# Rows of three graphs by index transfers through HBM instead of one-hot matmuls, in a graph-attention and mixture-of-experts kernel

## The reference, cut to what matters

```python
def per_graph(x, a):                       # 4 graphs of 256 rows; a = layernorm(x), 256 x 256
    h = gat_layer(x, a, W0, ...)           # twice: feat = x W; softmax(leaky(e) - 1e10*(1-a)) @ feat; + b; elu
    return gat_layer(h, a, W1, ...)
x = x + tanh(g_xattn) * gat(ctx, layernorm(x))
# then a mixture of experts over the 1024 rows of layernorm(x):
logits = tanh(xt @ Wg1.T) @ Wg2.T          # 8 experts, the best 2 weighted by a softmax
h = silu(einsum('td,ehd->teh', xt, Wup) + bup)
out = einsum('te,teo->to', scores, einsum('teh,eoh->teo', h, Wdown) + bdown)
x = x + tanh(g_ffn) * out
```

## Time and profile before

| | before |
|---|---|
| time, median of 3 runs | 93.43 us (92.78 to 94.61) |
| profiled execution: its time | 93.16 us |
| profiled execution: its span | 91.4 us |
| PE busy, PEld busy | 83.3 us (91%), 78.1 us (85%) |
| DVE, ACT, POOL busy | 64.7 us (71%), 55.2 us (60%), 43.5 us (48%) |
| share of PE in the chain that ended last | 59%; DVE 17%, DMA 6%, issue 6%, ACT 5% |

### The profile page before, as it was taken

One profiled execution on the slowest core, in us unless ns is written; L12 is line 12 of the kernel. 1 busy time (PEld: TensorE's weight loads), 2 busy tenths in 40 slices (PEclk: granted clock), 3 DMA queues, 4 the chain that ended last, 5 costly groups with the idle time before them and its releaser, 6 DMA issues.

```text
span 91.4 us, 1958 instructions
## 1 busy us (share of the span) xinstructions
PE 83.3 (91%) x615; PEld 78.1 (85%) x615; DVE 64.7 (71%) x202; ACT 55.2 (60%) x132; POOL 43.5 (48%) x95
## 2 busy tenths in 40 slices
PE   4959999989999999999999999999999999999800
PEld 4728888869899999989998999999999999999700
DVE  5887797857897609998599368795359767899520
ACT  1446888596695948398927799763366564433100
POOL 7970953698003999925900002885002988800000
PEclk9999999999999999999999999999999999999998
DMA  1999991000000000000000000030000030003021
GB/s 34 286 273 400 405 386 60 0 0 0 7 4 0 0 0 0 7 0 4 0 0 0 7 0 0 4 115 4 7 0 0 0 115 0 0 7 115 4 84 56
DMA packets 3339, 5.44 MB, mean 60 GB/s; under 512 B 474, under 2 KB 2748, under 8 KB 3068
## 3 DMA queue, kind: packets, MB, share of 16 engines
q1 hardware_dynamic: 3164, 5.00, 16.0%
q10 hardware_dynamic: 160, 0.26, 1.1%
HBM read 4.21 MB, written 1.05 MB: 58 GB/s over the span
## 4 chain that ended last, share of the span: by engine, by line
PE 59%; DVE 17%; DMA 6%; issue 6%; ACT 5%; DVEq 1%; POOL 1%; ACTq 1%
PE bank L734 6%; DMA ctx_sb<-in_ctx_t 6%; PE bank L735 6%; PE bank L739 6%; PE bank L896 6%; PE bank L781 5%; PE bank L872 5%; PE bank L783 5%; PE bank L782 5%; DVE hid_lo L1093 4%; PE bank L859 3%; PE bank L756 3%; DVE hid L1085 2%; PE bank L679 2%; DVE stat L990 2%
## 5 line engine op out<-in xcount | busy, mean ns | idle before, releaser
L1085 DVE TENSOR_TENSOR hid<-act_sb,bank 128x256 f32<-128x256 f32 x32 | 13.4, 418 | 10.9 <-PE bank L756 9.0
L518 ACT ACTIVATE act_sb<-bank,small_sb 128x256 f32<-128x256 f32 x32 | 15.1, 471 | 8.7 <-PE bank L739 8.4
L526 ACT CAST hid_hi<-hid 128x256 fp32r<-128x256 f32 x32 | 13.0, 405 | 10.7 <-DVE hid L1085 9.7
L781 PE MATMUL bank<-wdown_hi,hid_hi 128*128 128x256 f32 x64 | 18.4, 287 | 0.3 <-ACT hid_hi L526 0.3
L734 PE MATMUL bank<-xt_hi,wup_hi 128*128 128x256 f32 x64 | 18.0, 304 | 0.1
L783 PE MATMUL bank<-wdown_hi,hid_lo 128*128 128x256 f32 x64 | 18.1, 282 | 0.0
L782 PE MATMUL bank<-wdown_lo,hid_hi 128*128 128x256 f32 x64 | 18.0, 281 | 0.0
L735 PE MATMUL bank<-xt_hi,wup_lo 128*128 128x256 f32 x64 | 16.6, 281 | 0.0
L1093 DVE TENSOR_TENSOR hid_lo<-hid,hid_hi 128x256 fp32r<-128x256 f32 x32 | 13.4, 420 | 0.2
L739 PE MATMUL bank<-xt_lo,wup_hi 128*128 128x256 f32 x64 | 12.7, 280 | 0.0
L734 PEld LDWEIGHTS bank<-xt_hi,wup_hi 128*128 128x128 f32 x64 | 12.1, 189 | 0.5 <-ACT act_sb L518 0.3
(11 more groups left out here) (147 smaller groups left out, 180.6 us busy)
## 6 DMA issues: line engine op xcount, KB each, us to landing
x_sb<-in_x SPq DMA_DIRECT2D x4, 256.0 KB, 5.1
wup_sb<-in_wup SPq DMA_DIRECT2D x1, 1024.0 KB, 7.2
wdown_sb<-in_wdown SPq DMA_DIRECT2D x1, 1024.0 KB, 9.4
out<-out_sb SPq DMA_DIRECT2D x3, 256.0 KB, 2.2
check_sb<-in_check_w SPq DMA_DIRECT2D x1, 320.0 KB
w_sb<-in_w SPq DMA_DIRECT2D x1, 256.0 KB, 5.5
out<-out_sb SPq DMA_DIRECT2D x2, 128.0 KB, 2.5
ctx_sb<-in_ctx_t ACTq DMA_DIRECT2D x1, 192.0 KB, 5.6
```

Source lines behind the costliest of these rows:

```text
L518: nc.scalar.activation(act_out(n), bank[:, UP[n % 2], 0:N], ACT.Silu, bias=bup_sb[:, k % E:k % E + 1]).then_inc(silu_rdy, 1)
L526: nc.scalar.copy(hid_hi[:, n % HID_SLOTS, :], hid[:, n % 2, :]).then_inc(hid_hi_rdy, 1)
L781: nc.tensor.matmul(dst, hid_hi[:, n % HID_SLOTS, part], wdown_hi[:, e, :], start=False, stop=False, skip_group_check=True)
L1085: nc.vector.tensor_tensor(hid[:, n % 2, :], act_out(n), bank[:, PICK[n % 2], 0:N], ALU.mult).then_inc(hid_rdy, 1)
```

## The change

Graph 0 keeps its one-hot matrices. For graphs 1 to 3 they are gone, with `turn`, `turned`, `twice_part`, `source_copy` and `gather` of these graphs. In their place:

- DVE's `rows_leader` gives the index of each row's maximum (two MAX_INDEX of 256 columns for each graph). SP writes the indices to HBM (`leader_out`). POOL reads them back at the indices themselves (`leaders`, two index transfers), which gives leader[leader[i]].
- SP writes z of the graph to HBM (`z_out`, 256 KB), and POOL fetches its rows at these indices (`fetch`, two index transfers of 128 rows of 1 KB).
- `gated(b)` waits for these rows instead of a matmul, and reads them from SBUF instead of PSUM. `gated(1)` moves from ahead of DVE's round 0 to round 0, `gated(2)` from round 0 to round 10, `gated(3)` from round 5 to round 12, each with its statistics.
- POOL's list is ordered anew. The six one-hot passes and the four low parts of wdown leave it; the latter go to DVE, in rounds 3, 5, 7 and 8.
- On SP the load of wdown comes after the second `leader_out`, and the loads for the safety check come after the last `z_out`.
- The first four products use four banks instead of two.
- ACT makes all four high parts of wup ahead of the second layer's graph 1. `act_norm` of the next graph moves from e = 2 to e = 4, `pe_xt` and its splits from e = 4 to e = 6; both tiles of graph 0's `xn` are made on DVE; its gate and its difference of logits (ACT) move into rounds 1 and 2; `pe_score` of graph 0 moves from round 3 to round 5.

The core of the diff:

```diff
-SCORE_PLACE = (3, 6, 6, 6)
+SCORE_PLACE = (5, 6, 6, 6)
...
+            def leader_out(b):
+                sp.wait_ge(leader_rdy, C * b)
+                sp.dma_start(leader_hbm[b - 1][:].rearrange("(c p) k -> p c k", p=P), leader[:, pair(b), :]).then_inc(leader_st[b - 1], 16)
+
+            def z_out(b):
+                sp.wait_ge(z_rdy, b + 1)
+                sp.dma_start(z_hbm[b - 1][:].rearrange("(c p) d -> p c d", p=P), elu_exp[:, b, :, :]).then_inc(z_st[b - 1], 16)
+
+            leader_out(1)
+            leader_out(2)
+            sp.dma_start(wdown_sb[:], wdown).then_inc(wdown_ld, 16)
+            leader_out(3)
+            z_out(1)
+            z_out(2)
+            z_out(3)
...
+            def leaders(b):
+                pool.wait_ge(leader_st[b - 1], 16)
                 for t in range(C * b, C * b + C):
+                    nc.gpsimd.indirect_dma_start(leader2[:, t, :], None, leader_hbm[b - 1][:],
+                                                 bass.IndirectOffsetOnAxis(leader[:, t, 0:1], 0)).then_inc(leader2_ld[b - 1], 16)
+
+            def fetch(b):
+                pool.wait_ge(leader2_ld[b - 1], 16 * C)
+                pool.wait_ge(z_st[b - 1], 16)
+                for t in range(C):
+                    nc.gpsimd.indirect_dma_start(rows[:, b - 1, t, :], None, z_hbm[b - 1][:],
+                                                 bass.IndirectOffsetOnAxis(leader2[:, C * b + t, 0:1], 0)).then_inc(rows_ld[b - 1], 16)
...
+            leaders(1)
+            wup_part(0)
+            row_power(pool, 0, 0)
+            wup_part(1)
+            wup_part(2)
+            fetch(1)
+            wup_part(3)
+            leaders(2)
+            row_power(pool, 0, 1)
+            leaders(3)
+            fetch(2)
+            fetch(3)
+            row_power(pool, 0, 2)
+            scores(pool, 0, 1)
             row_power(pool, 0, 3)
-            scores(pool, 0, 1)
...
+            return (UP + PICK)[n] if n < 4 else UP[n % 2]
...
-                if e == 4 and b + 1 < B:
+                if e == 6 and b + 1 < B:
                     pe_xt(pe, run, b + 1)
...
-            pe_experts(pe, 0, {1: [lambda: gather(2)], 4: [lambda: gather(3)]})
+            pe_experts(pe, 0, {})
...
-            dve_experts(dve, 0, {0: [lambda: gated(2), lambda: dve_stats(dve, 0, 2)], 
-                                 5: [lambda: gated(3), lambda: dve_stats(dve, 0, 3)], 13: [check_peaks],
+            dve_experts(dve, 0, {0: [lambda: gated(1), lambda: dve_stats(dve, 0, 1)],
+                                 3: [lambda: wdown_part(0)], 5: [lambda: wdown_part(1)], 7: [lambda: wdown_part(2)], 8: [lambda: wdown_part(3)],
+                                 10: [lambda: gated(2), lambda: dve_stats(dve, 0, 2)],
+                                 12: [lambda: gated(3), lambda: dve_stats(dve, 0, 3)], 13: [check_peaks],
```

229 lines of the change are left out of this document (89 added, 140 removed).

## The result

| | before | after |
|---|---|---|
| time, median | 93.3 us (4 runs, 92.78 to 94.61) | 102.52 us (4 runs, 102.04 to 104.65) |
| ratio after / before | | 1.097, 95% interval 1.091 to 1.103 |
| profiled execution: span | 91.4 us | 100.2 us |
| PE busy | 83.3 us | 83.7 us |
| DVE, ACT, POOL busy | 64.7, 55.2, 43.5 us | 70.9, 53.5, 45.3 us |

The changed kernel is 9.7% slower. The forecast was 92.7 us, with 90.4 to 95.0 as its range: it was wrong in sign and by far in size. Ratios compare the fast executions of both kernels; medians and ranges count all of them.

What follows compares the result with a forecast made beforehand. PE was taken to bound from 49.2 us, DVE's chain before it; some 7.2 us leave PE, but round 8's 2.8 us lead shrinks to 0.5: 93.16 - 0.5 = 92.7 us, range 90.4 to 95.0.

Steps and rivals of the forecast that it cites:

- The lead of 2.8 us at round 8: Start of round 8: forecast at 33.0 us, against 35.77 before, a lead of 2.8 us.
- rival of the lock: Graph 0's norm on DVE held by POOL's wup pass: 1.1 us late, total 93.8 us; chance 0.10.
- The price of the clock: PE idle from 28.1 to 31.2, clock falls to 1.2 GHz: some 1.5 us, total 94.2 to 94.7; chance 0.10.
- rest hidden: Clock rival: beyond the transposes, two products, a pick and the gate (some 1.5 us), half speed adds nothing to the path.
- DVE's sum for rounds 8 to 15: From graph 1's second `hid` to the end of `score_t`: 12.7 us of DVE work, shrinking the lead to 0.5 us.
- The way through HBM: Graph 1's rows: z lands at 22.0, two index transfers of 1.0 us each, landing 2.2; rows there at 26.2.
- the 27.0 that it had for the route: End of graph 0's route on DVE, ahead of `gated(1)`: forecast at 27.0 us, hiding the rows by 0.8 us.
- The rival of late rows: At `fetch(1)`, index transfers dearer than taken: rows up to 30.0, total up to 95.7 us; chance 0.18.
- z of graph 1 at 19.8: End of `elu1(1)`, behind graph 0's powers, DVE's norms and small casts: forecast at about 19.8 us.
- the forecast of 48.6: End of graph 1's `score_t` on DVE: forecast at 48.6 us, against 49.07 before.
- POOL's second queue: `scores(1)` behind graph 2's powers ends at 45.8 and round 16 starts at 47.6: again about half a microsecond of lead.
- The rule on starved descriptors: POOL's index transfers: DVE's two-port passes starve descriptor writing, one fetch 2.5 us late, total 94.4 us.

Runs made afterwards that it cites:

- e3: Changed kernel with POOL's wup low parts reordered off DVE's norm, plus idle PE matmuls at four pauses: 96.28 us, ratio 1.031 to the kernel before.
- e1: Changed kernel with idle PE matmuls (18, 30, 10 and 8) at four pauses to keep the clock up: 98.52 us, ratio 1.055 to the kernel before.
- e9: e7 without the last two idle-matmul groups, graph 3's sums back in round 12, the peaks' reductions moved to round 6: ratio 1.005 to the kernel before.
- e4: Changed kernel with two banks for all products instead of four for the first four: 101.89 us, ratio 1.088 to the kernel before.
- e5: e3 with graph 3's gating sum and statistics moved from DVE's round 12 to 17: ratio 1.030 to the kernel before.
- e7: e3 with the moves of both e5 and e6: ratio 1.028 to the kernel before.
- e12: Kernel before with the peaks' six reductions moved from DVE's round 13 to round 0: 92.72 us, ratio 0.993 to the kernel before.
- e6: e3 with graph 2's gating sum and statistics moved from round 10 to 9, second fetch ahead of third leader transfer: ratio 1.036 to the kernel before.

## Why the prediction was wrong, point by point

Two steps of the prediction failed, and a third came out too small. The lead of 2.8 us at round 8 was a lag of 0.8, because POOL's passes held three instructions of DVE on graph 0's path (the prediction's rival of the lock, 1.1 us; 2.2 by e3 against e1). The price of the clock, 1.5 us with the "rest hidden", was 4.0 by e1. DVE's sum for rounds 8 to 15 was the right bound, but 12.7 us of it took 13.8 with the clock held.

- *The way through HBM, right in its prices, hidden by luck.* Index transfers: 0.94 to 1.23 us on POOL each, 0.30 between two, where I took 1.0. Landing of z 2.0 us in the changed kernel (2.2 taken). But the fetch of graph 1 began at 24.12 and not at 22.0, so by the prediction's own terms its rows came at 28.6, 1.6 us behind the 27.0 that it had for the route. They were hidden only because the route was later still. Where graph 0's route had been made faster, `gated(1)` did wait for them, in seven runs, by 0.20 to 1.15 us (0.87 in e3, 0.47 in e9). The rival of late rows was there, behind a larger loss.
- *Graph 0, wrong in its timing.* The step "z of graph 1 at 19.8" failed: `elu1(1)` ended at 21.2. I had this as the rival of the lock, at 1.1 us and a chance of 0.10. The order made it likely, and the place could be read in it: before, POOL's `rows_onehot(3)` stood between graph 0's powers and the next low part of wup, and the change removed it, so that the pass moved to 17.84, onto the norm. The size was wrong too: three instructions of DVE were held, not one, by 1.0, 1.1 and 1.4 us.
- *The end of the route, 29.75 instead of 27.0.* `gate_prod` began at 25.23 (24.1 forecast), and the route took 4.5 instead of 2.9; 1.4 of the difference is the lock again, on `ldiff`. Together with the late `gate_prod`, these are the 2.75 us. Without the lock the walk was right: counted from the start of graph 0's powers it has the end of the route 9.8 us later, e3 has 9.9, and the changed kernel 12.9.
- *The lead at round 8, 2.8 us forecast, a lag instead:* graph 1's transposes began at 34.41, not at 31.2, and round 8's product at 36.58, 0.8 after that of before, not at 33.0. The terms: the route 2.75 late, powers 1.4 instead of 1.1, and four transposes and a product of PE at half clock, 1.09 and 1.43 us, where 0.45 and 0.71 had been taken.
- *The clock, the mechanism right, the size wrong by far.* I saw one of the two pauses, from 28.1 to 31.2, priced it at 1.5 us and gave it 0.10. The error is in "rest hidden": I took the clock to be low for the gate and two products. It was low for over 13 us, and at half speed PE is the bound of rounds 8 to 10. And I did not see that it could fall a second time, behind rounds 14 to 16. It cost 4.0 us in e1. The Trainium skill (TensorE: Matmul & The Clock Gate, Part 1) has it that an idle array loses its clock: the trace agrees at 30 us, where the granted clock went to 0.50 at the end of a pause of 2.38 us. At 57 us it fell 1.9 us into busy work, behind pauses of 1.34 and 1.00 us, and e4 had the same pauses without the fall.
- *DVE's 12.7 us as the bound of rounds 8 to 15, right in kind, too short and too early.* In the changed kernel the stretch began at 41.58 and not at 35.85, and took 14.35 us: it ended 7.3 us behind the forecast of 48.6, and 5.7 of these were lost before it began. With the clock held it took 13.8 (e1, e3), of which 0.62 is a wait of DVE for ACT that the sum did not have. It followed the work put in it: 2.0 us less made it 1.7 to 1.8 shorter (e5, e7), and the exchange of e9 0.3. So with lock and clock both mended (e3) the change still lost 3.4 us from round 8's pick to round 17's (18.55 instead of 15.16), where the forecast had the lead shrink by 2.3. e12 does not speak against it: in the kernel before PE was the bound, busy for 13.16 of 13.40 us.
- *POOL's second queue, seen, but no second proof.* "POOL has `scores(1)` now behind the powers of graph 2" was priced at 45.8, no loss. It was 52.1: the statistics on which the powers wait came at 47.0 and not at 40.7, as round 10 itself was late. The queue hangs on DVE's, so its agreement with the sum confirmed nothing; and e6, which brought it forward by 0.85 us, moved nothing.
- *The rule on starved descriptors.* The Trainium skill (SBUF — State Buffer, "Who interferes with whom") speaks of descriptor writing starved by DVE's passes, which by the prediction's estimate would have made a fetch 2.5 us late. No index transfer of the changed kernel took POOL more than 1.23 us (1.42 in e6, the longest of all), so this case does not show it. The same section says that a DVE pass in a two-port mode, or with two inputs in SBUF, and POOL shut each other out. The trace agrees: the norm, the cast and `ldiff` were held by 1.0, 1.1 and 1.4 us.
